# Last experts of a two-layer gated block: second-half results scattered by token instead of gathered by token

## What is computed

```python
g = softmax(layer_norm(h) @ router_w.T)          # 4 experts
top2_w, top2_idx = top_k(g, 2)
hid = relu(layer_norm(einsum('bsd,edh->bseh', h, w1)))
expert_out = einsum('bseh,ehd->bsed', hid, w2)
out = sum(take_along_axis(expert_out, top2_idx) * top2_w)
x = x + tanh(g_ffn[1]) * layer_norm(out)
```

## Time and profile before

| | |
|---|---|
| median of 3 runs | 891.08 us (890.73 to 892.11) |
| the profiled execution, its own time | 888.89 us |
| its span in the profile | 886.9 us |
| last stage, from its first instruction to the end of the span | about 706 to 887 us |
| last block's result out of PSUM | 854.6 us |
| mean granted TensorE clock | 0.916 of full speed |

### The profile page before, as it was taken

How to read it: one execution, slowest core, us unless ns; L and a number is a source line. 1 busy time by engine, 2 the same in 40 slices (tenths; PEclk the granted TensorE clock), 3 DMA queues, 4 the chain that set the end, 5 groups by cost and what they waited for, 6 DMA issues and landing times. The chain is left out here.

```text
span 886.9 us, 21023 instructions
## 1 busy us (share of the span) xinstructions
PE 726.0 (82%) x6871; PEld 548.3 (62%) x6871; DVE 594.9 (67%) x1432; ACT 464.7 (52%) x953; POOL 458.5 (52%) x592
## 2 busy tenths in 40 slices
PE   3789999999987598989999998478798379997820
PEld 2456666666665498988777777367686246665510
DVE  5566777777785669884445542678867356667766
ACT  3546666766655468673333331344454247776632
POOL 5788788798600438881000002665833518655555
PEclk9879999999999579999999998797979689999975
DMA  6326444442300428764222223785521214323233
GB/s 174 93 71 148 112 112 118 122 108 74 81 14 2 144 60 295 244 208 129 85 83 79 84 73 89 205 229 166 146 70 44 77 35 139 96 81 95 84 92 104
DMA packets 87662, 98.94 MB, mean 112 GB/s; under 512 B 17260, under 2 KB 77132, under 8 KB 87564
## 3 DMA queue, kind: packets, MB, share of 16 engines
q1 hardware_dynamic: 63468, 66.10, 25.3%
q0 software_dynamic: 16432, 24.66, 10.3%
q10 hardware_dynamic: 7664, 6.89, 2.6%
HBM read 61.03 MB, written 24.38 MB: 96 GB/s over the span
## 5 line engine op out<-in xcount | busy, mean ns | idle before, releaser
L782 DVE TENSOR_REDUCE a_mx<-ps 112x2 f32<-112x750 f32 x128 | 120.2, 939 | 49.9 <-PE ps L400 48.0
L672 POOL DMA_DIRECT2D a_stkK<-a_KS x248 | 119.3, 489 | 19.2 <-issue 14.8
L642 ACT ACTIVATE a_Pf<-ps 125x672 f32<-125x672 f32 x128 | 90.0, 729 | 11.2 <-PE ps L344 9.9
L51 PE MATMUL ps<-f_w2hi,f_hh 128*128 (+1 forms) x292 | 80.3, 275 | 4.0 <-issue 2.8
L51 PE MATMUL ps<-f_w2lo,f_hh 128*128 (+1 forms) x292 | 80.2, 275 | 0.0
L51 PE MATMUL ps<-f_w2hi,f_hl 128*128 (+1 forms) x292 | 80.2, 275 | 0.0
L1841 POOL MEMSET a_half<- 112x2 f32 x1 | 0.1, 94 | 143.7 <-POOLq L88 143.7
L1547 DVE CAST f_hh<-ps 128x512 bf16<-128x512 f32 x41 | 28.4, 692 | 64.4 <-PE ps L1283 64.4
L2453 POOL TENSOR_TENSOR f_rl<-f_rf,f_rh 128x512 bf16<-128x512 f32 x34 | 39.5, 1161 | 59.8 <-DVE f_rh L2521 59.3
L2397 ACT ACTIVATE f_rf<-ps,f_ln 128x128 f32<-128x128 f32 x136 | 54.4, 452 | 25.7 <-PE ps L2348 25.7
L1207 POOL DMA_INDIRECT f_xd<-xn,pos x32 | 54.4, 1700 | 22.9 <-issue 22.9
(11 more groups left out here) (392 smaller groups left out, 2270.5 us busy)
## 6 DMA issues: line engine op xcount, KB each, us to landing
a_raw<-F_w SPq DMA_DIRECT2D x22, 512.0 KB
f_xg<-f_xd SPq DMA_DIRECT2D x75, 128.0 KB
f_yd<-f_yo SPq DMA_DIRECT2D x75, 128.0 KB
f_raw<-F_w SPq DMA_DIRECT2D x14, 512.0 KB
a_ctxF<-ctxT SPq DMA_DIRECT2D x16, 375.0 KB, 3.5
a_cR<-ctx SPq DMA_DIRECT2D x16, 375.0 KB
a_stkK<-a_KS POOLq DMA_DIRECT2D x248, 23.4 KB, 2.0
f_xd<-a_zero ACTq DMA_DIRECT2D x13, 384.0 KB, 3.2
```

What stands on the lines that cost most here:

```text
L51: ins = nc.tensor.matmul(out, l, r, start=first and i == 0, stop=last and i == len(steps) - 1)
L642: nc.scalar.activation(Pf[:, j % PB], psST[:C, j % 2, :, 0:SC * T], ACT.Exp, scale=DH ** -0.5).then_inc(exp_done, 1)
L672: pool.dma_start(stkK[SIDE * h + DH * a:SIDE * h + DH * (a + 1), w.slot, jj], KS[2 * DH * jj + DH * h:2 * DH * jj + DH * (h + 1), w.odd, p ...
L782: nc.vector.reduce_max(mx[:, n.odd, j // JJ, :, j % JJ], maxima_of(n, j)[:T, :, :S], AX).then_inc(mx_red, 1)
```

## The change

It touches the way of the second half's rows only; the first half is scattered, computed and gathered as before, apart from when.

- **Rows carry their address.** `xn` becomes `xn_wide` with 258 floats per token; the two extra ones hold 2 x (the token's number in the half). A new DRAM tensor `xw` of 17 x 128 rows x 258 floats takes the second half's sorted rows (1032 bytes a row) in place of the second half of `xd`. The rows of expert choice i = 0 are scattered first (8 scatters), then POOL waits until they have landed, adds 1 to the address column, waits for that, and scatters the rows of i = 1.
- **Unused rows.** `xw` is filled beforehand, in `l0_attention` at batch 12 (`ROWS_AT`) on ACT's queue: one DMA of zeros (2176 rows of 1024 bytes) and one of addresses of spare rows (2176 pieces of 8 bytes). POOL makes these by one iota, DVE converts them.
- **In the steps of the second half** (blocks 17 to 33) DVE copies the address of the block's 128 rows into an int32 tile (`row_numbers`, one copy of 128x1 behind `x_low`), and POOL sends the block's result with one indirect scatter (`send`) into a table `yt`, row 2 x token + i. Stores to `yd` of these blocks go away.
- **The end.** SP waits for the last sends and loads each of the 8 batches with one plain DMA (112 partitions x 2 KB). The 16 gathers go away. The last block's send is put ahead of the last two gathers of the first half.
- **Order.** First-half gathers are one a step in steps 21 to 36 instead of two in every second step; combines come one step later (24, 26, ...), the last two of the first half behind the loop's last block.

```diff
+HB = B // 2
+NB1 = (2 * HB * T - E1 - (2 * HB * T - E1) % P) // P + E1
+SPARE = 2 * HB * T
-        self.xn = self.sb("xn", [T, B, D], F32)
+        self.xn_wide = self.sb("xn", [T, B, D + 2], F32)
+        self.xn = self.xn_wide[:, :, 0:D]
...
 # l0_attention, ACT
                             fill(b)
+                            if isinstance(b.b, int) and b.b == ROWS_AT:
+                                act.wait_ge(spare_set, 1)
+                                act.dma_start(blank_rows[:, :, 0:D], zero[:].unsqueeze(1).broadcast_to([P, NB1, D])).then_inc(k.rows_filled, 16)
+                                act.dma_start(blank_rows[:, :, D:], spare[:]).then_inc(k.rows_filled, 16)
 # l0_attention, POOL and DVE
+                nc.gpsimd.iota(spare_i[:], pattern=[[P, NB1]], base=SPARE, channel_multiplier=1).then_inc(spare_made, 1)
+                nc.vector.tensor_copy(spare[:], spare_i[:].unsqueeze(2).broadcast_to([P, NB1, 2])).then_inc(spare_set, 1)
 # l1_attention, POOL and DVE
+                        nc.gpsimd.iota(row_i[:], pattern=[[2 * T, HB]], base=0, channel_multiplier=2).then_inc(iota_done, 1)
+                        nc.vector.tensor_copy(k.xn_wide[:, HB:, D:], row_i[:].unsqueeze(2).broadcast_to([T, HB, 2])).then_inc(made, 1)
 # l1_experts
-        STEPS = range(-2, BLOCKS + 5)
-        GATHER, COMBINE = NB1 + 4, NB1 + 6
-        STORE = NB1 + 11
+        STEPS = range(-2, BLOCKS + 6)
+        GATHER, COMBINE = NB1 + 4, NB1 + 7
+        STORE = NB1 + 12
 # l1_experts, SP
-                        sp.dma_start(xg[:, b % RING, :], xd[b * P:(b + 1) * P, :]).then_inc(xg_in[b % RING], 16)
+                        at_least(sp, rows_read, b - RING - NB1 + 1)
+                        if b < NB1:
+                            sp.dma_start(xg[:, b % RING, 0:D], xd[b * P:(b + 1) * P, :]).then_inc(xg_in[b % RING], 16)
+                        else:
+                            sp.dma_start(xg[:, b % RING, :], xw[(b - NB1) * P:(b - NB1 + 1) * P, :]).then_inc(xg_in[b % RING], 16)
-                    if d >= 0:
+                    if 0 <= d < NB1:
                         sp.wait_ge(y_out, d + 1)
                         sp.dma_start(yd[d * P:(d + 1) * P, :], yo[:, d % 3, :]).then_inc(y_st[d % 3], 16)
...
+                for i in range(3):
+                    sp.wait_ge(y_sent[i], 16 * sent(i, BLOCKS))
+                for j in range(HB, B):
+                    at = 2 * T * (j - HB)
+                    sp.dma_start(yg[:, j], yt[at:at + 2 * T, :].rearrange("(t i) d -> t i d", i=2)).then_inc(yg_in[j], 16)
 # l1_experts, POOL
-                rows = [(i, b) for b in range(HB, B) for i in range(2)]
+                rows = [(i, b) for i in range(2) for b in range(HB, B)]
+                def send(m):
+                    pool.wait_ge(y_out, m + 1)
+                    pool.wait_ge(rows_read, m - NB1 + 1)
+                    nc.gpsimd.indirect_dma_start(
+                        out=yt, out_offset=bass.IndirectOffsetOnAxis(rows_of[:, m - NB1:m - NB1 + 1], 0),
+                        in_=yo[:, m % 3, :], in_offset=None, bounds_check=SPARE + NB1 * P - 1, oob_is_err=True).then_inc(y_sent[m % 3], 16)
...
+                    if len(rows) == HB:
+                        pool.wait_ge(k.dispatched, 16 * 3 * HB)
+                        nc.gpsimd.tensor_tensor(k.xn_wide[:, HB:, D], k.xn_wide[:, HB:, D], f1.ones[:, 0:1].broadcast_to([T, HB]), ALU.add).then_inc(second_rows, 1)
+                        pool.wait_ge(second_rows, 1)
                     if n >= SCATTER and rows:
                         scatter(*rows.pop(0))
                         scatter(*rows.pop(0))
...
-                    if gathers_of(n) is not None:
-                        j = gathers_of(n)
-                        if j == 0:
+                    m = block_at(n - 2)
+                    if m == BLOCKS - 1:
+                        send(m)
+                    if 0 <= n - GATHER < 2 * HB:
+                        if n == GATHER:
                             for i in range(3):
                                 pool.wait_ge(y_st[i], 16 * len(range(i, NB1, 3)))
-                        gather(j)
-                for i in range(3):
-                    pool.wait_ge(y_st[i], 16 * len(range(i, BLOCKS, 3)))
-                for j in range(HB, B):
-                    gather(j)
+                        gather((n - GATHER) // 2, (n - GATHER) % 2)
+                    if m is not None and NB1 <= m < BLOCKS - 1:
+                        send(m)
 # l1_experts, DVE
+                def row_numbers(g):
+                    dve.wait_ge(xg_in[g % RING], 16 * (g // RING + 1))
+                    nc.vector.tensor_copy(rows_of[:, g - NB1:g - NB1 + 1], xg[:, g % RING, D:D + 1]).then_inc(rows_read, 1)
...
                         x_low(g)
+                        if g >= NB1:
+                            row_numbers(g)
```

More of the change, by code:

```diff
@@ L147, in l0_attention @@
         zero = sb("zero", [P, D], F32)
+        spare_i, spare = sb("sparei", [P, NB1], mybir.dt.int32), sb("spare", [P, NB1, 2], F32)
+        spare_made, spare_set = k.sem("a0_sparemade"), k.sem("a0_spareset")
         ONES = 200
@@ L159, in l0_attention @@
         FILL = -(-NBLK // B)
+        ROWS_AT = 12
+        blank_rows = xw.rearrange("(n p) d -> p n d", p=P)
         early = ExitStack()
@@ L659, in _ @@
                     rows_high(LAST, t)
+                act.wait_ge(k.rows_filled, 32)
             @block.gpsimd
@@ L1684, in bases @@
     link(tt(f.base[:], f.incl[:], f.nblk[:], ALU.subtract))
-    link(ts(f.base[:], f.base[:], float(P), float(h * NB1 * P), ALU.mult, ALU.add))
+    link(ts(f.base[:], f.base[:], float(P), None, ALU.mult))
 def places(nc, f, link, h):
@@ L2264, in l1_experts @@
         RING, AHEAD = 4, 6
-        xg = sb("xg", [P, RING, D], F32)
+        xg = sb("xg", [P, RING, D + 2], F32)
+        rows_of = sb("rowsof", [P, NB1], mybir.dt.int32)
+        rows_read, second_rows = sem("rowsread"), sem("secondrows")
+        y_sent = [sem(f"ysent{i}") for i in range(3)]
         xgT = [sb(f"xgT{p}", [P, 2, KD, P], BF16) for p in ("hi", "lo")]
@@ L2288, in l1_experts @@
         block_at = lambda n: n if 0 <= n < BLOCKS else None
-        STEPS = range(-2, BLOCKS + 5)
+        STEPS = range(-2, BLOCKS + 6)
         GATES, RANK, PLACE, SCATTER = 0, 1, 2, 3
-        GATHER, COMBINE = NB1 + 4, NB1 + 6
-        gathers_of = lambda n: (n - GATHER) // 2 if n >= GATHER and (n - GATHER) % 2 == 0 and (n - GATHER) // 2 < HB else None
+        GATHER, COMBINE = NB1 + 4, NB1 + 7
         first_of = lambda n: (n - COMBINE) // 2 if n >= COMBINE and (n - COMBINE) % 2 == 0 and (n - COMBINE) // 2 < HB else None
         second_of = lambda n: first_of(n - 1)
-        STORE = NB1 + 11
+        STORE = NB1 + 12
+        gathered = lambda j: 32 if j < HB else 16
+        sent = lambda i, end: len([m for m in range(NB1, end) if m % 3 == i])
         with nc.Block(no_gpsimd_drain=True) as block:
@@ L2408, in first @@
                         act.wait_ge(gates_done, 1)
-                    act.wait_ge(yg_in[j], 32)
-                    nc.scalar.activation(acc[:, j, :], yg[:, 0, j, :], ACT.Copy, scale=f1.gate[:, 0, j:j + 1]).then_inc(first_done, 1)
+                    act.wait_ge(yg_in[j], gathered(j))
+                    nc.scalar.activation(acc[:, j, :], yg[:, j, 0, :], ACT.Copy, scale=f1.gate[:, 0, j:j + 1]).then_inc(first_done, 1)
                 def last_deviation(j):
@@ L2524, in out @@
                     dve.wait_ge(y_full, m + 1)
-                    if m >= 3:
+                    if 3 <= m < NB1 + 3:
                         dve.wait_ge(y_st[m % 3], 16 * (m // 3))
+                    elif m >= 3:
+                        dve.wait_ge(y_sent[m % 3], 16 * sent(m % 3, m - 2))
                     nc.vector.tensor_copy(yo[:, m % 3, :], k.ps[:, 4 + m % 2, 0:D]).then_inc(y_out, 1)
                 def combine(j):
-                    dve.wait_ge(yg_in[j], 32)
+                    dve.wait_ge(yg_in[j], gathered(j))
                     dve.wait_ge(first_done, j + 1)
-                    stt(acc[:, j, :], yg[:, 1, j, :], f1.gate[:, 1, j:j + 1], acc[:, j, :], ALU.mult, ALU.add).then_inc(sum_done, 1)
+                    stt(acc[:, j, :], yg[:, j, 1, :], f1.gate[:, 1, j:j + 1], acc[:, j, :], ALU.mult, ALU.add).then_inc(sum_done, 1)
                     dve.wait_ge(sum_done, j + 1)
@@ L2599, in build @@
         yd = nc.dram_tensor("f0_yd", (NBLK * P, D), F32, kind="Internal").ap()
-        l0_attention(nc, k, a, xd)
+        xw = nc.dram_tensor("f1_xw", (NB1 * P, D + 2), F32, kind="Internal").ap()
+        l0_attention(nc, k, a, xd, xw)
         k.release()
@@ L2611, in build @@
         if stages >= 4:
-            y1 = nc.dram_tensor("f1_yd", (2 * NB1 * P, D), F32, kind="Internal").ap()
-            l1_experts(nc, k, a, f1, xd, y1)
+            y1 = nc.dram_tensor("f1_yd", (NB1 * P, D), F32, kind="Internal").ap()
+            yt = nc.dram_tensor("f1_yt", (SPARE + NB1 * P, D), F32, kind="Internal").ap()
```

(1 more changed line is left out.)

32 lines of the change are left out of this document (16 added, 16 removed).

## The result

| | before | changed |
|---|---|---|
| median | 892.18 us (20 runs, 883.40 to 894.13) | 894.93 us (20 runs, 888.07 to 900.26) |
| the profiled execution, own time | 888.89 us | 897.04 us |
| its span | 886.9 us | 895.2 us |
| mean granted TensorE clock | 0.916 | 0.911 |

The ratio is 1.0036, 95% interval 1.0019 to 1.0054: slower, against a forecast of 890.0, and outside the range of 887.0 to 893.8. That matters for every difference taken from these profiles.

The account below looks back on a forecast made before the run. Before the last block's result POOL, DVE and PE limit alternately; the tail is set by POOL's gathers. Terms -4.0 + 0.7 + 0.5 + 1.3 + 0.4 = -1.1 took 891.08 to 890.0 us, range 887.0 to 893.8.

Parts of the forecast that it names:

- the term of +0.4: First attention and moved work: the fill's issues hidden on ACT; its traffic, iota and cast cost +0.4 us, from 0 to +2.
- -1.1: Whole kernel: the forecast's sum of all terms in us, from a median of 891.08 to 890.0.
- Rival C: First attention: the fill's traffic makes keys come late, 3 us lost, 893 us; chance 0.08.
- The tail: Behind the last block: gathers replaced by plain loads, eight batches at DVE's pace; -4.0 us, bounds -4.6 and -3.0.
- The pause: Step 7, between scatter rounds: POOL waits for landing, adds 1, waits for the result; +0.7 us, bounds 0.5 and 1.5.
- The copies: Steps 15 to 31: 17 address copies on DVE, partly showing, cost +0.5 us in all.
- rival B: Last stage: DVE's address copies are held until POOL's low lets go; 894.9 or 892.2 us; chance 0.18.
- The sends: POOL, steps 19 to 34: one send a step, showing in steps 19 to 24; +1.3 us, bounds +0.3 and +2.0.
- rival A: Last stage: the loop absorbs sends and copies and the fill is hidden; -3.0 us, 888.1; chance 0.29.
- The baseline: Whole kernel: starting point was a profiled execution of 888.89 us, with the median shown 2.2 above it, 891.08.

Follow-up runs that it names:

- e11: The changed kernel with the DMA of addresses issued at turn 14, not right behind that of zeros at turn 12; 892.25 us, ratio 1.0001 (0.9972 to 1.003).
- e8: e3 with SP issuing the eight table loads only when the first half's last gather has landed; one run, own time 896.05 us.
- e5: e3 with the last block's send behind the first half's last two gathers instead of ahead; 893.64 us, ratio 1.0003 (0.9975 to 1.0032).
- e3: The changed kernel with the fill as six DMAs of whole 1032-byte rows, spread over turns 12 to 15; 892.0 us, ratio 0.998 (0.9952 to 1.0009).
- e6: e3 with the first half's gathers two steps earlier and add_beta twice a step from step 11; 887.19 us, ratio 0.9958 (0.9928 to 0.9987).
- e7: e6 with the second scatter round one step later and two add_beta in step 7; 886.26 us, ratio 0.9926 (0.9898 to 0.9954).
- e9: The kernel before plus four DMAs on ACT's queue: addresses alone in turns 11 and 13, zeros twice in turn 15; 893.4 us, one run.

## Why the prediction was wrong

- **The step that failed** is "An issue took 0.39, and ACT's next work waited 0.80 for PE anyway: hidden, as is the spare cast." The price was read from a DMA that is first in its turn. Two large ones came behind it, and the third took 3.44. ACT stood for 4.40, PE waited 3.06 for it, and the term of +0.4 was +4.5, and this alone turns -1.1 into +3.0. Rival C named the place and the loss (3 us, 893) and had 0.08. It put it down to late transfers of keys or maxima; here it was ACT's queue first, and the late transfer showed only in e11, when the issue was out of the way. That 13 fills of 384 KB (the prediction says 14) left no wait was no evidence for 2.2 MB at once.
- **The tail** was right in kind and mis-sized: -2.7 instead of -4.0, short even of its bound of -3.0. Send, gathers, DVE's pace and the loads' start were as forecast; combine(8) came 1.8 late, 1.5 of it from the last gather, 4.57 instead of 3.04 because eight loads run beside it (without them e8 has 2.85 and e5 2.74); DVE's pace behind it gave 0.6 back. The 3.04 of the earlier trace rows was measured with nothing beside it but other gathers. The change's own device, the last send first, cuts both ways: with the send last (e5) the tail is 1.8 shorter than e3's.
- **The pause** was +1.42, near its upper bound, where I took 0.7. The add's 0.21 is near my lower price; the 0.80 from POOL's result to POOL's own next DMA had no row before, and I had put 0.3 into the upper bound for it. The terms given for that bound, 0.26, 0.72 and 0.3, add up to 1.28 and not to 1.5, so by its own terms the bound was passed.
- **The copies** cost 0 (forecast 0.5), and rival B is false: all 17 took 0.142 to 0.145, 13 of them beside POOL's `low`. The Trainium skill, "VectorE: DVE Perf Modes", section "Mode 2×_2P", has a copy use its second port only where its outermost dimension that is not one is even (or odd and equal in source and destination), and a 128x1 copy has no such dimension. The trace agrees with 0.144 against 2.60 for the 112x24 cast. DVE's gap was there, and taking 0.5 for "waits" had no row under it.
- **The sends** cost +0.6 to 0.7 in steps 19 to 25 of the changed kernel's profile, and 0.3 to 0.4 came back up to Y. Steps 21, 22 and 23 took 4.39, 4.38 and 4.39 as forecast, POOL without a gap; steps 19 and 20 lost nothing, and step 24 took 4.35 and not 4.76. This last is not the rule: in e3, e5, e8 and e11, with the same order there, step 24 took 4.92 to 4.93 and steps 19 to 25 together 24.99 to 25.04, +1.2 against the first profile, of which at most 0.3 came back. In step 24 of those four the combine's scaled sum took 1.93 to 2.03 and ran into POOL's `low`, where the changed kernel's profile has 0.47, over before `low` starts. So the 1.3 was about right, and rival A holds at most in the changed kernel's own profile.
- **The baseline.** The sum was made against a profile that lies 3.3 under the median of 20 runs, and 2.2 of that was known. By itself this is an error of 1.1.

Measured terms, all from the changed kernel's profile: 4.5 + 1.4 + 0 + 0.4 - 2.7 = +3.6, against +2.75 in the medians and +3.3 in the table; with the fill put right, e3's ratio is 0.998 (0.9952 to 1.0009), which neither tells a gain from none nor from the -1.1 forecast. The change's idea pays once the fill is in six DMAs and the gathers are out of the loads' way (e6, 0.9958); without the standing wait on POOL as well (e7) it is 0.9926, and the two are not told apart.

## What to carry to other kernels

A DMA's issue is work of the engine that issues it, and its price is not that of a lone one: put large ones on a queue one by one, here half a turn or more apart, and not behind each other in an engine's busy stretch. A landing time read where nothing else runs is a lower bound; ask what the change itself starts beside it. And before differences of a few us are taken from one profile, look how far its own time lies from the median: here some slower scatters 300 us before the change's stage were worth more than the forecast's whole effect.

## What the hardware showed that I had not expected

- On ACT's queue a DMA of 2176 rows of 1 KB issued in 0.37 us with nothing in its turn before it (e9) and in 0.60 to 0.78 behind the usual fill, but behind another such DMA in 3.25. One of 2176 pieces of 8 bytes took 3.44 and 3.56 behind such a DMA, 0.64 and 1.76 behind the usual fill and 0.37 alone.
- During and behind a stall of ACT of 4.40 us, in which PE waited 3.06, stood three windows of 4 us at a granted clock of 0.63, 0.50 and 0.59; turn 13, behind the stall, was 0.66 longer (15.65 against 14.99).
- From a POOL tensor instruction's end to the start of POOL's own indirect DMA that waits for its result passed 0.80 us.
- An indirect gather of 112 rows was used 2.74 to 3.04 us behind its start with no loads beside it (e5, e8, before), and 4.57 to 5.21 beside eight loads of 224 KB (four profiles).
- A DVE sum of two SBUF tiles that took 0.47 with no POOL arithmetic beside it took 2.01 where POOL's `low` and `add_beta` ran beside it (e3, step 24), while the 128x1 copies beside `low` kept their 0.144.
